# Query and key columns by heads in the attention of a graph network on Trainium2

## The reference, cut to what matters

```python
q = (h @ Wq + bq).reshape(n, HD, HEADS) * scaling      # HD = 32, HEADS = 8
k = (h @ Wk + bk).reshape(n, HD, HEADS)
v = (h @ Wv + bv).reshape(n, HD, HEADS)
s = jnp.einsum('edh,edh->eh', q[rows], k[cols])        # one score for each edge and head
m = jax.ops.segment_max(s, rows, num_segments=n)
e = jnp.exp(s - m[rows])
z = jax.ops.segment_sum(e, rows, num_segments=n)
out = jax.ops.segment_sum((e / z[rows])[:, None, :] * v[cols], rows, num_segments=n)
```

## Time and profile before

| | |
|---|---|
| median of 3 runs | 8035.07 us (8003.05 to 8042.56) |
| span of the profiled execution, first to last instruction | 8020.0 us |
| the profiled execution's own time | none is given beside its span |
| PE busy | 5048.0 us, 63% |
| DVE busy | 3676.9 us, 46% |
| POOL busy | 3410.2 us, 43% |
| ACT busy | 2138.1 us, 27% |
| granted TensorE clock, mean | 0.776 of 2.4 GHz |

### The profile page before, as it was taken

The page is one execution under the profiler, slowest core; times in us unless marked ns, Lnnn a source line. Parts: engine busy times, 40 slices in busy tenths (PEclk is TensorE's granted clock), DMA queues, the critical chain, the costliest instruction groups (busy, mean ns, idle before and its releaser), DMA issues. The chain is left out here.

```text
span 8020.0 us, 86247 instructions
## 1 busy us (share of the span) xinstructions
PE 5048.0 (63%) x22204; PEld 3739.6 (47%) x22204; DVE 3676.9 (46%) x7463; ACT 2138.1 (27%) x5299; POOL 3410.2 (43%) x3736
## 2 busy tenths in 40 slices
PE   4663656665665665666567999998454545454444
PEld 3442444444444444444446888886333333333333
DVE  4554666666666666666664444443121212122211
ACT  2332333333333333333334555554000000000000
POOL 1114444444444444444440000001666666666666
PEclk8776777787777877777778999999666666666666
DMA  5224444444444444444443444444333333333333
GB/s 99 109 105 115 129 138 139 129 133 139 128 134 137 133 131 139 135 129 138 137 122 143 192 187 193 187 192 170 105 101 103 105 101 105 103 103 100 105 103 96
DMA packets 464813, 1041.01 MB, mean 130 GB/s; under 512 B 169809, under 2 KB 262393, under 8 KB 439689
## 3 DMA queue, kind: packets, MB, share of 16 engines
q0 software_dynamic: 237248, 726.98, 31.6%
q1 hardware_dynamic: 166736, 310.21, 10.4%
q10 hardware_dynamic: 60792, 3.40, 0.9%
HBM read 743.19 MB, written 295.32 MB: 129 GB/s over the span
## 5 line engine op out<-in xcount | busy, mean ns | idle before, releaser
L634 POOL DMA_INDIRECT kvg<-kv_rows,index x1666 | 1595.0, 957 | 1985.7 <-PE sum_ps L898 1455.6
L1350 POOL DMA_INDIRECT msg_in<-msg_rows,index_c x1666 | 1595.3, 958 | 879.4 <-issue 503.9
L1406 PE MATMUL sum_ps_c<-msg_in,hot 128*128 128x256 f32 x3332 | 1124.9, 490 | 1144.1 <-issue 573.2
L1406 PEld LDWEIGHTS sum_ps_c<-msg_in,hot 128*128 128x128 f32 x3332 | 817.2, 250 | 1437.9 <-issue 1099.8
L656 DVE TENSOR_TENSOR kvg<-kvg,qe_ps 128x512 f32<-128x512 f32 x833 | 567.5, 681 | 1289.6 <-remote 850.3
L887 PE MATMUL qe_ps<-q_win,onehotT 128*128 128x256 bf16 x4998 | 903.1, 351 | 219.0 <-DVE kvg L656 214.8
L1368 DVE SCALAR_TENSOR_TENSOR result<-sums_c,x_in 128x256 f32<-128x256 f32 x119 | 50.4, 424 | 1929.4 <-ACT sums_c L1394 1697.7
L887 PEld LDWEIGHTS qe_ps<-q_win,onehotT 128*128 128x128 bf16 x4998 | 583.6, 123 | 482.3 <-issue 238.1
L662 DVE TENSOR_REDUCE score<-kvg 128x112 f32<-128x3584 f32 x119 | 786.6, 6610 | 0.0
L898 PE MATMUL sum_ps<-kvg,onehot 128*128 128x264 f32 x3332 | 779.8, 392 | 4.1 <-DVE kvg L731 4.1
L898 PEld LDWEIGHTS sum_ps<-kvg,onehot 128*128 128x128 f32 x3332 | 637.9, 195 | 112.9 <-DVE kvg L731 5.6
(11 more groups left out here) (183 smaller groups left out, 6511.1 us busy)
## 6 DMA issues: line engine op xcount, KB each, us to landing
msg_rows<-msg SPq DMA_DIRECT2D x196, 1024.0 KB, 3.9
kvg<-kv_rows,index POOLq DMA_INDIRECT x1666
msg_in<-msg_rows,index_c POOLq DMA_INDIRECT x1666
kv_rows<-kv POOLq DMA_DIRECT2D x98, 256.0 KB, 2.3
q_win<-q_rows SPq DMA_DIRECT2D x119, 192.0 KB
q_rows<-q POOLq DMA_DIRECT2D x98, 192.0 KB, 2.3
agg_rows<-sums SPq DMA_DIRECT2D x119, 132.0 KB
x_in<-x_rows SPq DMA_DIRECT2D x119, 128.0 KB
```

What stands on the lines that cost most here:

```text
L634: pool.indirect_dma_start(out=kv[u][:, t, 0:2 * D], out_offset=None, in_=kv_rows, in_offset=bass.IndirectOffsetOnAxis(ap=index[u][:, t:t + 1],
L1350: pool.indirect_dma_start(out=msg[u][:, t, :], out_offset=None, in_=msg_rows, in_offset=bass.IndirectOffsetOnAxis(ap=index[u][:, t:t + 1], ...
L1406: last = nc.tensor.matmul(sum_ps[u][:, :], hot[u][:, t, :], msg[u][:, t, :], start=t == 0, stop=t == B - 1 and isinstance(i, int) and i == 0)
```

## The change

The columns of Wq and Wk and the elements of bq and bk are reordered in the chip's memory from d * 8 + h to h * 32 + d. q and k then lie by heads in `q_rows`, `kv_rows`, `qe_ps` and in the products, and the reduction of line 662 reads 32 neighbours for each score in place of 32 elements that lie 8 apart (32 bytes). v keeps its order. The reordering is done where the weights are split: the copy of line 294 becomes four (for each half of the rows, one of 512 columns of q and k in the new order and one of 256 of v), the subtraction of line 395 becomes four likewise. The biases are loaded into two new tiles and written by heads by two DVE instructions.

```diff
+def heads_apart(ap):
+
+    return ap.rearrange("p (g h d) -> p g h d", h=H, d=HD)
+
+
+def heads_inside(ap):
+
+    return ap.rearrange("p (g d h) -> p g h d", h=H, d=HD)
...
+        b_q_in = sb("b_q_in", [P, D])
+        b_k_in = sb("b_k_in", [P, D])
...
-            sp.dma_start(b_q[:, :], bq.partition_broadcast(P)).then_inc(weights_in, 16)
-            sp.dma_start(b_kv[:, 0:D], bk.partition_broadcast(P)).then_inc(weights_in, 16)
+            sp.dma_start(b_q_in[:, :], bq.partition_broadcast(P)).then_inc(weights_in, 16)
+            sp.dma_start(b_k_in[:, :], bk.partition_broadcast(P)).then_inc(weights_in, 16)
...
-            nc.scalar.copy(w_hi[:, :, :], w_all[:, :, :]).then_inc(w_hi_got, 1)
+            for c in range(C):
+                nc.scalar.copy(heads_apart(w_hi[:, c, 0:2 * D]), heads_inside(w_all[:, c, 0:2 * D])).then_inc(w_hi_got, 1)
+                nc.scalar.copy(w_hi[:, c, 2 * D:3 * D], w_all[:, c, 2 * D:3 * D]).then_inc(w_hi_got, 1)
...
-                    pe.wait_ge(w_lo_got, 1)
+                    pe.wait_ge(w_lo_got, 2 * C)
...
-            nc.vector.tensor_scalar(b_q[:, :], b_q[:, :], HD ** -0.5, None, ALU.mult).then_inc(bias_scaled, 1)
-            dve.wait_ge(bias_scaled, 1)
+            nc.vector.tensor_scalar(heads_apart(b_q[:, :]), heads_inside(b_q_in[:, :]), HD ** -0.5, None, ALU.mult
+                                    ).then_inc(bias_scaled, 1)
+            nc.vector.tensor_copy(heads_apart(b_kv[:, 0:D]), heads_inside(b_k_in[:, :])).then_inc(bias_scaled, 1)
+            dve.wait_ge(bias_scaled, 2)
...
-            dve.wait_ge(w_hi_got, 1)
-            nc.vector.tensor_tensor(w_lo[:, :, :], w_all[:, :, :], w_hi[:, :, :].bitcast(F32),
-                                    ALU.subtract).then_inc(w_lo_got, 1)
+            dve.wait_ge(w_hi_got, 2 * C)
+            for c in range(C):
+                nc.vector.tensor_tensor(heads_apart(w_lo[:, c, 0:2 * D]), heads_inside(w_all[:, c, 0:2 * D]),
+                                        heads_apart(w_hi[:, c, 0:2 * D].bitcast(F32)), ALU.subtract).then_inc(w_lo_got, 1)
+                nc.vector.tensor_tensor(w_lo[:, c, 2 * D:3 * D], w_all[:, c, 2 * D:3 * D],
+                                        w_hi[:, c, 2 * D:3 * D].bitcast(F32), ALU.subtract).then_inc(w_lo_got, 1)
...
-                nc.vector.tensor_reduce(score[:, :, :], kv[u][:, :, 0:D].rearrange("p t (d h) -> p h t d", h=H), AX.X,
+                nc.vector.tensor_reduce(score[:, :, :], kv[u][:, :, 0:D].rearrange("p t (h d) -> p h t d", h=H), AX.X,
```

More of the change, by code:

```diff
@@ L1582, in body @@
                     dve.wait_ge(weighed, WEIGH_STEPS * k + 3)
-                    nc.vector.tensor_reduce(score[:, :], prod[:, :].rearrange("p (d h) -> p h d", h=H), AX.X,
+                    nc.vector.tensor_reduce(score[:, :], prod[:, :].rearrange("p (h d) -> p h d", h=H), AX.X,
                                             ALU.add).then_inc(weighed, 1)
```

## The result

The changed kernel took 8091.73 us (8075.26 to 8110.13, 4 runs) beside 8038.82 us (8003.05 to 8046.32, 4 runs) of the kernel before on the same chip: a ratio of 1.0082 [1.0059, 1.0104], so 0.8% slower. I had forecast 8028 us and no difference. The profiled execution took 8075.26 us with a span of 8073.7, 1.6 us more than its span. Two executions of later experiments took far longer than all others of their kernel (11,753 us in e3, 14,704 us in c1) and are left out of every ratio.

A forecast was written before the change was run, and what follows sets the result against it. A chain of waits in attention, a 30.65 us ring tied to the gathers' traffic, was taken as the bound. Three ungated blocks -8 and setup +2.3 gave about -6 on the 8035.07 median: 8028 us, range 7880 to 8060.

The forecast's parts named there:

- The reduction's duration: Score reduction on DVE in attention: from 6.61 to 3.9 us, 2.7 us saved per block.
- The setup: Weight split before the first tile: one copy and one subtraction become four each, +2.3 us, range 0.5 to 4.
- Why PE's word reaches DVE so late the trace doesn't say: Attention: the products wait though PE's matmuls were long done; the prediction left the cause of the late release open.
- the gate: Attention: end of the gathers' traffic, to which product 3's release is tied, 20.0 us after the first gather in block 46.
- all four rivals: Third product gets through 22%, 7890; reduction on the path 12%, 7716; slower 8%, 8380; reduction isn't faster 3%, 8037.
- the held ring: Attention block: first gather, 20.0 us, the gate, 10.6 us, next first gather; 30.65 us, with the reduction not on it.
- The reduction is on the path: Rival, 12%: the gate hangs on DVE's pace in attention, so 119 x 2.7 = 321 us are saved: 7716.
- Product 2 and 3 wait for their release as before: Attention: an earlier reduction moves products 0 and 1 sooner, not 2 and 3, adding 1.1 to 2.7 us of DVE idle.
- 0 us for some 116 blocks: Attention: nothing on the 30.65 us ring is shortened, so most blocks save nothing; only three blocks save, 8 us.
- The slower rival: Rival, 8%: product 1 is caught too, so product 2's word comes only with the gate, 3 us a block: 8380.
- The third product getting through: Rival, 22%: earlier matmuls let one more product through before the gate in most blocks, 1.2 us each: 7890.
- The idle time before the products: DVE idle before line 656 in attention, 1289.6 us, expected up by about 119 x 2 us.

The follow-up runs named there:

- e3: The kernel before, its reduction taking only 18 of the 32 elements of each head: 6361.84 us, 0.9644 of the kernel before at 6595.93 us.
- c1: The changed kernel, its reduction taking only 12 of the 32 elements of each head: 8025.36 us, 1.0025 of the kernel before at 8004.55 us.
- e1: The changed kernel, its reduction reading elements 8 apart again: 6601.89 us, 1.0009 of the kernel before at 6595.93 us.
- h1: The changed kernel as it is, run again: 8018.75 us, 1.0020 of the kernel before at 8004.32 us.
- h2: The changed kernel, its reduction reading elements 8 apart again: 8010.56 us, 1.0005 of the kernel before at 8004.32 us.
- a2: The kernel before, unchanged, run again for its trace: 6609.73 us in one run.

## Why the prediction was wrong, point by point

**The reduction's duration** was right: 3.9 us worked out, 3.864 measured, and the groups' 460 us against 464. Also the wide step as its cause: e1 differs in the step alone and loses all the gain (1.0009 against 0.9651).

**The setup** was right: +2.3 us worked out, 2.25 measured. ACT does pay for the wide step, 1.11 us for 512 elements against 0.40 for 256 neighbours.

**"Why PE's word reaches DVE so late the trace doesn't say"** was where the argument should have stopped to put a chance on it. I took the gate for a property of the kernel: the release of product 3 bound to the end of its own gathers' traffic. It doesn't belong to the program alone: whole sets of executions have it and whole sets don't. In free executions the same gathers run, 1.25 us apart, and product 3 comes 4.9 us after product 0. The forecast and all four rivals were built on the held ring. "The reduction is on the path" (12%, 7716, 4% less) comes near what a free execution shows, 3.5% less, of 6,600 us, but not by its own words: it let the gate hang on DVE's pace, and in a free execution there is no gate. It also overpriced the saving, by leaving out that the gathers become the limit after 2.0 of the 2.7 us.

**"Product 2 and 3 wait for their release as before"**, and from it "0 us for some 116 blocks", is the step that failed in the comparison that was forecast. Product 3 does wait as before (19.62 and 19.78 us). Product 2 doesn't: it is released behind the gate in 46 blocks in place of 13, and takes the back transposes and products 4 to 6 along. Product 0 came sooner as said, even by 1.95 us on average in place of 1.1 (3.79 us after the first gather against 5.74), but product 1 by only 0.2 (7.17 against 7.36), and product 2 came 0.6 us later. The step took the release time of product 2 as given by the gathers, though block 46 had shown a fixed end for product 3 alone. The ring grew by 0.47 us, and 116 x 0.47 = 55 us against 52.9 measured.

**The slower rival** named this direction with too many blocks and too high a price. It priced product 2 behind the gate at 3 us in all blocks, 350 us, with product 1 caught as the trigger. That is what happened in 9 blocks, at 2.1 us each, and block 45 above is one of them. In 24 more blocks than before product 2 was caught by itself, which no rival had, at 0.58 us. A third part, 0.18 us in the uncaught blocks, stands in no rival and has no cause shown.

**The third product getting through** (22%, 7890) shows in part without paying: in h1 25 blocks have product 3 within 2.5 us of the start of the last gather, over 1 us ahead of the usual 3.5, where in h2 16 have, and product 3 comes 0.57 us earlier on average, but product 6 doesn't.

**The idle time before the products** was to rise by 119 x 2 = 238 us and rose by 357, the 327 us of the reduction and 30 us of the longer ring.

**Not reckoned with**: the stretch from product 6 to the next gather, with the same work in it, took 0.08 to 0.34 us a block more where the reduction was short. Only in c1 does the clock differ enough beside it to be a likely cause.

## What to carry to other kernels

A wait whose releaser the profile can't name may not belong to the kernel: before building a ring on it, look whether what should have released the engine was long done, and price the change once with that wait and once without, since the two can differ in sign (here +0.8% and -3.5%). A second chip, and an execution without records, are worth a run before such a wait is optimized for. Work saved on an engine that then only waits isn't sure to be neutral: it moves the engine's requests earlier, into a stretch where they can be caught. Where the saving is real, ask for the next limit, here the 17.5 to 18.7 us that POOL needs to issue 14 gathers.

## What the runs showed of the hardware

**One program, two paces.** With no difference in the program the kernel before took 8,004 to 8,039 us in three sets of runs (with the first comparison) and 6,591 to 6,604 in four. In the held ones the mean granted clock is 0.776 against 0.842, DVE's instructions take as long (0.681 and 0.679 us a product), and what is late is the signals from PE. The trace of the kernel before shows it in block 46: PE's matmuls for products 2 and 3 end at 2051.72 and 2052.38, the updates of their semaphore are recorded at 2058.36 and 2064.84, and the products start 0.03 and 0.02 us later. The gate is the end of the gathers' traffic: the last packet of a block's gathers ends 3.4 us after the start of the last gather (median of 100 blocks), product 3 starts at 3.7 us. SyncE's instructions slow down too while the gathers run. Its queue in the kernel before, held, then free (a2):
```profile
2056.19 0.01 SPq L597 DMA_DIRECT2D agg_rows<-sums  x1
2063.33 0.02 SPq L603 DMA_DIRECT2D index<-src_idx  x1
```
```profile
2038.44 0.35 SPq L597 DMA_DIRECT2D agg_rows<-sums  x1
2039.01 0.51 SPq L603 DMA_DIRECT2D index<-src_idx  x1
```
Between these two issues of SP's program lie 7.1 us held and 0.57 free, but the held pair shown is among the longest and has the end of the loop in between. Like against like, the median is 5.74 against 0.92 us with the end of the loop between them and 2.94 against 0.57 without. Of 1,809 register instructions of SP in attention 559 take over 0.3 us held, most of them some 0.7, and none does free; of the other engines' none does in either. The second layer's gathers show the same: `collect` takes 20.4 us a block held and 17.6 free. What holds the signals isn't known. The sets fit a property of the chip (8, 1 and 10 free, 9 and 4 held), but only chip 1 was used twice, so they don't prove it.

The held traces also lack semaphore records. Counted in the packed traces, a held execution has 37,441 to 38,569 of them and a free one 91,211 to 91,305, with all instructions and DMA packets there in both. Up to the first gather of attention the two agree (6,786 in the kernel before, 6,787 in a2). The landings of attention's gathers, 16 to each of 1,666, are 26,656; a2 has 26,602 of them and the held kernel before 6,115. Every execution of this case was recorded, so no run says whether the hold is there without records, and the recording itself stays a rival. The Trainium skill (NOTIFIC — the notification-queue block, §7.1 "Overflow: three behaviours, one of which stalls the engine") says that in one of three settings a full ring of records stalls the engine that produces them until software drains it. That would fit the late signals, though not the missing records, and no run here shows it.

**The step of a reduction.** DVE's tensor_reduce over 3,584 fp32 elements took 6.61 us with elements 32 bytes apart and 3.864 with neighbours, 1.84 and 1.08 ns an element.
